# Attention 1 of a fused two-layer kernel: ScalarE copies one exponential later, users of PSUM bank 0 spread out, weighted values in two pieces, one maximum reduction for two blocks

## The reference

```
def _L1_attn_ref(x, Wq, Wk, Wv, Wout):
    q = jnp.einsum('bld,dhe->blhe', x, Wq)
    k = jnp.einsum('bld,dhe->blhe', x, Wk)
    v = jnp.einsum('bld,dhe->blhe', x, Wv)
    a = jnp.einsum('bqhd,bkhd->bhqk', q, k) / Dh ** 0.5
    a = jnp.where(tril, a, NEG_INF)
    a = jax.nn.softmax(a, axis=-1)
    o = jnp.einsum('bhqk,bkhd->bqhd', a, v)
    return jnp.einsum('blhe,hed->bld', o, Wout)
```

## Time and profile before

| | |
|---|---|
| time, median of 3 runs | 933.88 us (930.04 to 935.28) |
| time of the profiled execution | 932.55 us |
| its span, first to last instruction | 930.8 us, so 1.75 us lie around it |
| mean granted TensorE clock | 0.980 |
| busy over the span | PE 91%, PEld 60%, DVE 78%, ACT 57%, POOL 50% |
| the eight periods of attention 1 | 396.1 to 659.4 us, 263.3 us |
| exponentials (L1877) | 160, 161.5 us, 1022 ns each |

### The profile page before, as it was taken

The page is one execution under the profiler, slowest core; times in us unless marked ns, Lnnn a source line. Parts: engine busy times, 40 slices in busy tenths (PEclk is TensorE's granted clock), DMA queues, the critical chain, the costliest instruction groups (busy, mean ns, idle before and its releaser), DMA issues. The chain is left out here.

```text
span 930.8 us, 17280 instructions
## 1 busy us (share of the span) xinstructions
PE 842.5 (91%) x5977; PEld 556.6 (60%) x5977; DVE 728.3 (78%) x1455; ACT 528.7 (57%) x771; POOL 465.4 (50%) x620
## 2 busy tenths in 40 slices
PE   5899999999778886689999999888889999999997
PEld 4677777775566655334444444443558767776875
DVE  6888998879899995888898998987666656565542
ACT  4677788789566675367777777767423223222311
POOL 4133222224568786236666666456464365345444
PEclk9999999999999999779999999999989999999999
DMA  9300000000000006765545446200000000000000
GB/s 284 93 12 12 11 11 11 0 13 0 16 1 12 1 12 130 142 129 117 111 82 126 106 85 127 52 4 14 12 1 24 1 23 23 23 0 23 11 12 12
DMA packets 36067, 43.79 MB, mean 47 GB/s; under 512 B 4878, under 2 KB 28094, under 8 KB 36000
## 3 DMA queue, kind: packets, MB, share of 16 engines
q1 hardware_dynamic: 36000, 42.93, 19.5%
HBM read 21.81 MB, written 15.09 MB: 40 GB/s over the span
## 5 line engine op out<-in xcount | busy, mean ns | idle before, releaser
L1877 ACT ACTIVATE PT<-PS 128x1024 f32<-128x1024 f32 x160 | 161.5, 1022 | 61.6 <-PE PS L1668 61.3
L1939 POOL TENSOR_SCALAR_AFFINE_SELECT PT<-PT 128x256 f32<-128x256 f32 (+1 forms) x224 | 97.3, 451 | 101.9 <-ACT PT L1877 99.9
L2368 POOL TENSOR_TENSOR PRE_sb<-PRE_sb,VA 128x512 f32<-128x512 f32 x64 | 82.3, 1285 | 125.8 <-DVE PRE_sb L2436 125.7
L2335 ACT ACTIVATE sg_d<-PS 128x512 f32<-128x512 f32 x64 | 38.1, 597 | 154.5 <-PE PS L1397 154.5
L2436 DVE TENSOR_TENSOR PRE_sb<-sg_d,PS 128x512 f32<-128x512 f32 x64 | 44.0, 688 | 79.6 <-ACT sg_d L2335 79.1
L465 ACT ACTIVATE E<-PS,m 128x512 f32<-128x512 f32 x128 | 85.7, 688 | 34.7 <-PE PS L351 25.8
L1979 DVE TENSOR_REDUCE negm<-PS 128x2 f32<-128x1024 f32 x64 | 77.8, 1221 | 20.0 <-PE PS L1657 19.6
L1684 PE MATMUL PS<-PT,VA 128*32 128x512 f32 (+3 forms) x1024 | 89.9, 446 | 3.6 <-POOL PT L1939 3.6
L1650 PE MATMUL PS<-kS,qS 52*128 52x384 bf16 (+3 forms) x512 | 64.3, 311 | 14.7 <-ACT PT L1877 6.9
L514 POOL TENSOR_SCALAR Qs<-Qs 128x1024 f32<-128x1024 f32 x32 | 34.5, 1080 | 81.6 <-ACT Qs L446 81.0
L1668 PE MATMUL PS<-qS,kS 55*128 55x384 bf16 (+3 forms) x512 | 63.4, 307 | 7.5 <-DVE negm L1979 3.5
(11 more groups left out here) (331 smaller groups left out, 2249.5 us busy)
## 6 DMA issues: line engine op xcount, KB each, us to landing
qk_rows<-parts SPq DMA_DIRECT2D x32, 192.0 KB, 2.8
qS<-qk_rows SPq DMA_DIRECT2D x32, 192.0 KB, 4.3
kS<-qk_rows SPq DMA_DIRECT2D x32, 192.0 KB, 4.6
xs_sb<-XN_sb SPq DMA_DIRECT2D x20, 256.0 KB, 2.3
qk_rows<-parts SPq DMA_DIRECT2D x32, 128.0 KB, 2.8
X_sb<-in_x_dram SPq DMA_DIRECT2D x8, 256.0 KB, 6.6
qk_rows<-parts SPq DMA_DIRECT2D x32, 64.0 KB, 2.5
out_dram<-X_sb SPq DMA_DIRECT2D x8, 256.0 KB, 2.3
```

The source lines that it names most:

```text
L1877: nc.scalar.activation(PT[:, quad % 2, u, :], PS[:, b:b + 2, :].rearrange("p b n -> p (b n)"), ACT.Exp).then_inc(exp_ready, 1)
L1939: nc.gpsimd.affine_select(out=v, in_=v, pattern=[[0, 4 if u == 4 else 2], [1, P]], compare_op=ALU.is_ge, fill=0.0, base=0, channel_multipl ...
L2368: nc.gpsimd.tensor_tensor(acts[:, s, f, :], acts[:, s, f, :], W[:, slot, s, :], ALU.mult).then_inc(weighted, 1)
```

## The change

Six edits, all inside `attention1`.

1. `weighted_v` has two calls a quad in place of three: kt = 0 after unit 3 (was unit 4), and kt = 1, 3, 2 together after unit 1 of the next quad (were kt = 1 after its unit 0, and kt = 3, 2 after its unit 1). The joint call waits for all seven masks.
2. `turn_ot` and VectorE's `divide` move from units (0,3) and (2,3) to (0,4) and (2,4), except in period 6. The users of bank 0 then come at (0,2), (0,4), (1,0), (1,2), (1,4), (2,0), (2,2), (2,4), (3,0), (3,2).
3. ScalarE's copies out of bank 0 and bank 7 stand one exponential later: `keep_ot` after E(0,2) and E(2,2), `keep_maxima` after E(0,3) and E(2,3), `keep_v` after E(1,1), `keep_on` after E(1,3), `keep` of q after E(2,1) and of k after E(3,3). `keep_x` stays after E(1,4).
4. VectorE reduces units 2 and 3 with one instruction over all four blocks of 128 in place of two (384 and 128 columns). `negm` gets three more slots for the parts, and `split_maxima` begins with one more linked instruction, the minimum over three slots.
5. `M_SLOT` exchanges the places of blocks 1 and 2 in `negm` and `mpart`; `turn_maxima` reads them in that order.
6. GpSimd's conversions for the staging move one unit later (the k part's second piece into the next period's unit (0,0)), and `factor` moves from after unit (1,0) to after (1,1).

```diff
-        negm = sb("negm", [P, NT, 2, NPAIR])
+        negm = sb("negm", [P, NT + 3, 2, NPAIR])
...
-                pe.wait_ge(masked, (i * 4 + quad) * 7 + {0: 2, 1: 6, 3: 7}[kts[0]])
+                pe.wait_ge(masked, (i * 4 + quad) * 7 + {0: 2, 1: 7}[kts[0]])
...
-                    if u == 4:
+                    if u == 3:
                         weighted_v(i, slot, quad, (0,))
...
-                    elif (quad, u) == (0, 3) and not first:
+                    elif (quad, u) == ((0, 3) if opens(i, 1) else (0, 4)) and not first:
                         pe.wait_ge(m_row, i * 2 + 2)
                         turn_ot(i - 1, 1)
...
-                    elif (quad, u) == (2, 3):
+                    elif (quad, u) == ((2, 3) if opens(i, 1) else (2, 4)):
...
-                    if u == 0 or u == 1:
-                        kts = (1,) if u == 0 else (3, 2)
+                    if u == 1:
                         if quad > 0:
-                            weighted_v(i, slot, quad - 1, kts)
+                            weighted_v(i, slot, quad - 1, (1, 3, 2))
                         elif not first:
-                            weighted_v(i - 1, 1 - slot, 3, kts)
+                            weighted_v(i - 1, 1 - slot, 3, (1, 3, 2))
...
-                    if (quad, u) == (0, 1) and not first:
+                    if (quad, u) == (0, 2) and not first:
                         keep_ot(i - 1, 1)
-                    elif (quad, u) == (0, 2):
+                    if (quad, u) == ((0, 2) if opens(i, 1) else (0, 3)):
                         keep_maxima(i, 1)
...
-                    elif (quad, u) == (2, 0) and ahead(i):
+                    elif (quad, u) == (2, 1) and ahead(i):
                         pr.keep(act, i + 3, 0, q_ready, qf_ready)
-                    elif (quad, u) == (2, 2) and not last:
+                    elif (quad, u) == (3, 3) and ahead(i):
+                        pr.keep(act, i + 3, 1, k_ready, kf_ready)
+                    if (quad, u) == (2, 2):
+                        keep_ot(i, 0)
+                    if (quad, u) == ((2, 2) if opens(i, 1) else (2, 3)) and not last:
                         keep_maxima(i + 1, 0)
...
-                    elif (quad, u) == (1, 0) and i > 1:
+                    elif (quad, u) == (1, 1) and i > 1:
                         factor(i - 2)
+                    elif (quad, u) == (0, 0) and behind(i):
+                        pr.second_part_on_pool(pool, i + 2, 1)
...
-                    nc.vector.tensor_reduce(negm[:, 2, :, pair], PS[:, b:b + 2, 0:384], AX.X, ALU.max, negate=True)
-                    ins = nc.vector.tensor_reduce(negm[:, 0, :, pair], PS[:, b:b + 2, 384:512], AX.X, ALU.max, negate=True)
+                    ins = nc.vector.tensor_reduce(negm[:, 0:4, :, pair].rearrange("p s r -> p r s"),
+                                                  PS[:, b:b + 2, :].rearrange("p b (s n) -> p b s n", n=P), AX.X, ALU.max, negate=True)
...
+                ch.link(nc.vector.tensor_reduce(negm[:, 3 + M_SLOT[2], :, hs], negm[:, 0:3, :, hs].rearrange("p s r a -> p r a s"), AX.X, ALU.min))
...
-                    elif (quad, u) == (2, 3):
+                    elif (quad, u) == ((0, 3) if opens(i, 1) else (0, 4)) and not first:
+                        divide(i - 1, 1)
+                    elif (quad, u) == ((2, 3) if opens(i, 1) else (2, 4)):
                         divide(i, 0)
```

More of the change, by code:

```diff
@@ L1487 @@
             [(0, 0, 1), (1, 0, 1), (2, 256, 1), (3, 256, 1)]]
+M_SLOT = (0, 2, 1, 3)
 def diagonal(bank, u):
@@ L1843, in _ @@
             in_periods(pe, period)
[L1844 to L1845 removed]
+            weighted_v(LAST, LAST % 2, 3, (1, 3, 2))
         @block.scalar
@@ L1877, in period @@
                     nc.scalar.activation(PT[:, quad % 2, u, :], PS[:, b:b + 2, :].rearrange("p b n -> p (b n)"), ACT.Exp).then_inc(exp_ready, 1)
-                    if (quad, u) == (0, 1) and not first:
+                    if (quad, u) == (0, 2) and not first:
                         keep_ot(i - 1, 1)
-                    elif (quad, u) == (0, 2):
+                    if (quad, u) == ((0, 2) if opens(i, 1) else (0, 3)):
                         keep_maxima(i, 1)
-                    elif (quad, u) == ((1, 1) if opens(i, 1) else (1, 0)) and not (first or last):
+                    elif (quad, u) == (1, 1) and not (first or last):
                         keep_v(i + 1, 1 - slot)
-                    elif (quad, u) == (1, 2) and not first:
+                    elif (quad, u) == (1, 3) and not first:
                         keep_on(i - 1)
@@ L1941, in period @@
                     if ahead(i):
-                        if (quad, u) == (2, 0):
+                        if (quad, u) == (2, 1):
                             pr.first_part_on_pool(pool, i + 3, 0, qf_ready)
-                        elif (quad, u) == (2, 1):
+                        elif (quad, u) == (2, 2):
                             pr.first_rest(pool, i + 3, 0)
-                        elif (quad, u) == (2, 2):
+                        elif (quad, u) == (2, 3):
                             pr.second_part_on_pool(pool, i + 3, 0)
@@ L1958, in period @@
                         (ex.low if part else ex.high)(pool, n)
-                    if (quad, u) == (1, 0) and first:
+                    if (quad, u) == (1, 1) and first:
                         factor_and_shift(nc, g, pool, 2 * LAST - 1, 2 * NB, 1, 2)
-                    elif (quad, u) == (1, 0) and i > 1:
+                    elif (quad, u) == (1, 1) and i > 1:
                         factor(i - 2)
+                    elif (quad, u) == (0, 0) and behind(i):
+                        pr.second_part_on_pool(pool, i + 2, 1)
                     elif (quad, u) == (0, 1) and behind(i):
@@ L2092, in period @@
                         split_maxima(i + 1, 0)
-                    if (quad, u) == (0, 3):
-                        if first:
-                            stats_of_last()
-                        else:
-                            divide(i - 1, 1)
-                    elif (quad, u) == (2, 3):
+                    if (quad, u) == (0, 3) and first:
+                        stats_of_last()
+                    elif (quad, u) == ((0, 3) if opens(i, 1) else (0, 4)) and not first:
+                        divide(i - 1, 1)
+                    elif (quad, u) == ((2, 3) if opens(i, 1) else (2, 4)):
                         divide(i, 0)
```

20 lines of the change are left out of this document (7 added, 13 removed).

## The result

The changed kernel takes 954.15 us (median of 4 runs, 953.45 to 955.06), the kernel before 933.08 on the same chip (4 runs, 930.04 to 935.28). The ratio is 1.023, with a 95% interval of 1.0192 to 1.0267. It is slower by 21 us, and outside my range of 927 to 944. The profiled execution took 953.75 us with a span of 951.9, against 932.55 and 930.8, at a granted TensorE clock of 0.971 against 0.980.

A forecast was written before the change was run, and what follows sets the result against it. TensorE (31.46 of 33.2 us busy) and VectorE (30.21) each nearly fill a full period. Growths of 0.5 + 1.2 + 1.5 + 0.5 + 1.7 = +5.4 us on 932.55 make 937.95; forecast 938.5, range 927 to 944.

The forecast's parts named there:

- TensorE's own work: Full period: 30.2 us of TensorE work, less 0.64 because each joint call takes 1.42 instead of 1.58.
- The waits at the quad's edge: Units (3,4) and (0,0) left bare, 0.95 together; (1,0) and (3,0) each wait 0.87 for `divide`, 1.74 a period.
- I cost both at 0: GpSimd's moved conversions and SyncE's later writes of the maxima: in time for their users, so no cost.
- a split of 1.1: VectorE's split with one more linked step, taken as 1.1 us; units (0,3) and (2,3) wait 0.39 and 0.53 behind it.
- My walk: One full period stepped through from S(0,2) to S(0,2): 3.9 us of waits, period 33.5, 0.3 longer.
- The edge periods: Growth forecast outside periods 1 to 4: period 0 +0.5, period 5 +1.5, period 6 +0.5, period 7 +1.7 us.
- My four terms for period 6: Lost cover before `project_v` +0.7, (1,4) -0.7, split before S(2,3) +1.0, the end -0.5: +0.5 us.
- my upper bound of 3: Period 7: forecast +1.7 us from a later first mask and other waits, bounds -1.5 and +3.
- B: Rival: even spacing pays, most of the waits at (1,0) and (3,0) go, faster at 927 us; chance 0.24.
- D: Rival: the joint call saves nothing because each kind pays its 0.16, 943 us; chance 0.13.
- C: Rival: saving and waits cancel, waits about 3.6 a period, periods 5 and 7 at most +1 together, 933.5 us; chance 0.21.
- The forecast's mechanism: Waits at the quad's edge cost more than the joint call saves: 938.5 us, own range 934.5 to 943; chance 0.42.

The follow-up runs named there:

- e2: Changed kernel with `turn_ot` and the division back at (0,3) and (2,3), `keep_maxima` back behind E(0,2) and E(2,2): 949.64 us, ratio 1.0182.
- e1: Changed kernel with GpSimd's second and third pieces of k moved from (0,0) and (0,1) to (0,2) and (0,3): 944.79 us, ratio 1.0103.
- e4: Kernel before with only kt = 0 put behind unit 3 and the joint call behind unit 1: 943.72 us, ratio 1.0109.
- e8: Changed kernel with the edits of e1 and e2 together: 943.12 us, ratio 1.0130.
- e7: Kernel before with only GpSimd's conversions of k moved one unit later, the second piece to (0,0): 931.25 us, ratio 1.0002.
- e11: e8 with GpSimd's `factor` back behind unit (1,0) in period 7: 941.96 us, ratio 1.0090.

## Why the prediction was wrong, point by point

**TensorE's own work: right.** The joint call was forecast at 1.42 and takes 1.43 between starts. The rule that I had weighed against it (the Trainium skill, TensorE: Matmul & The Clock Gate, Measured speedup vs the span model) would by an estimate leave it at some 1.57; here the measurement differs from the page and decides.

**The waits at the quad's edge: right in place, nearly in size.** M(0,0) 0.57 for a forecast of 0.62, the division 0.81 for 0.87, twice. What I mis-sized is the move's net worth: the waits that it replaces (0.57 each) stood in no term, so 1.74 of gross waits were 0.58 net in e2.

**"I cost both at 0", and a split of 1.1: the step that failed.** I looked whether the conversions end before their DMAs are wanted, and not at what runs on VectorE beside GpSimd. GpSimd's instructions hold the split's small steps, 0.97 becomes 2.60, and 1.24 us a full period follow (e1). My walk had the split at 1.1 and so S(0,3) waiting 0.39; the trace has `turn_maxima` waiting 1.00 and S(0,3) another 0.66. For (2,3) I had 0.53, and the trace has 0.41 and 0.66 from stretch 2 on. The missing term does not belong to edit 6 alone, where I had looked for it: edit 1 puts the third piece of k, which was not moved, beside the split's last step (e4), and edit 6 adds the second piece. With the falls of the clock that go with it, e1 takes 7.5 of the 11.6 us off that the four full stretches grew.

The rule was there to be read. The Trainium skill (SBUF — State Buffer, Who interferes with whom) says that a VectorE instruction with two SBUF inputs contends with a GpSimd instruction that reads SBUF, and a cast can do so in its two-port mode, and that whichever issues first has the shared pair of ports for the whole instruction while the other is blocked, while `tensor_reduce` never contends. The rows agree: GpSimd's instruction starts first each time, by 0.01 to 0.13 us, the casts and `tensor_tensor` steps end 0.03 to 0.06 us behind its end, and the `tensor_reduce` at 429.22 takes the 0.17 that it takes at 446.74, beside GpSimd's L825. No row shows the mode in which the casts ran.

**The clock: not in the sum at all.** I reckoned every distance at the full clock because the earlier trace rows shows 1.00 in the full periods. The same idle time that costs 1.66 us at (0,2) is followed in periods 3 and 4 by a fall of the clock, another 1.43 and 1.12, and in periods 1 and 2 by none. Falls also took part in stretches 6 (0.95) and 7 (0.88).

**The edge periods: right in sign, short in size.** Stretch 0 grew 1.4 for 0.5, 5 grew 2.2 for 1.5, 6 grew 2.0 for 0.5. Edit 1 alone does as much in 0 and 6 (e4: 1.6 and 2.9, with the clock at 0.93 and 0.95), and 1.6 in 5. My four terms for period 6 made 0.5, and edit 1 alone costs more there than all of them. Period 7 grew 5.2 for 1.7, beyond my upper bound of 3: I had the order right (factor, `apply`, selection), but no term for the clock, which was 0.88 there; at 0.99 and with `turn_ot` and the division back the growth is 2.6 (e2). The end of the period, where the last call waits 2.73 for its triangle (before, kt = 1 waited 1.79 there), was not tried by itself.

**The rivals.** B falls: the waits of 0.81 are there. D falls: the joint call takes 1.43. C would have needed waits of 3.6 a period; there were 6.1 in period 2 (35.7 less 29.6 of work). The forecast's mechanism holds, but as the smaller part of a growth of 22.4 where I had 5.4.

**What stays open.** What in stretch 6 costs 1.5 to 2.0 us with edit 1 (36.08 in the changed kernel at a clock of 0.95, 35.61 in e8 at 1.00, but 34.47 with edit 1 undone) was not read out step by step; nor was stretch 0. Stretch 1 is 0.78 shorter than stretch 2 in the changed kernel (in e8, too, 33.08 against 33.88): it lacks the waits of 0.41 and 0.66 at (2,2) and (2,3). From period 2 on `apply` stands in unit (1,4) ahead of the split at (2,0), and one cast of that split takes 0.47 instead of 0.18 beside GpSimd's L838; which of the two sets the waits was not tried alone. Nor was the changed kernel timed with edit 6 alone undone.

## What to carry to other kernels

When an edit changes when a job on GpSimd runs, by moving it or by moving what it waits for, read VectorE's timeline at the new time: it is not enough that it ends before it is wanted, since small VectorE steps in a linked chain can be held for the whole length of a GpSimd instruction. In a schedule where TensorE and VectorE both nearly fill the period, saved work can be worth nothing: here 0.64 us less a period made the kernel 0.8% to 1.1% slower, since units left bare wait 0.57 for an exponential and a GpSimd instruction meets the split (both in e4). What counts is which unit each cover stands on. An edit that is free alone (e7) can still add to a hold that another edit has made. A wait on TensorE can cost twice, once for itself and once for the clock behind it (here 1.66 us, and in some periods up to 1.43 more), and since a fall of the clock is not in every execution, compare stretches at the same granted clock before you credit an edit with the difference: e11 seemed to gain 2.3 us, and 2.2 of them were the clock.

## What the runs showed of the hardware

- A VectorE `tensor_tensor` over 128x32 took 0.19 alone and 1.10 beside a GpSimd `tensor_tensor` of 1.15; a cast of 0.18 took 0.43. A `tensor_reduce` over 128x24 beside another GpSimd `tensor_tensor` took its 0.17.
- After waits of 1.00 and 0.66 us close together TensorE's granted clock went to 0.50 in some periods and stayed at 1.00 in others with the same waits (periods 3 and 4, and 1 and 2, of the changed kernel). The same code in period 7 ran at 0.91 in one kernel's execution (e8) and at 0.99 in another's (e2), 2.2 us apart.
- A float32 call on four column groups takes some 0.16 beside its columns, with three, four or six blocks of 128 columns in it: 0.79, 1.00 and 1.43 between starts. Six blocks in one call take 1.43, in two calls 2 x 0.79.
